# Attention in a macaron block: reciprocal chain moved ahead, and three small TensorE products in other tile modes

## The reference

```
x = x + 0.5 * ffn(layernorm(x), w_gate, w_up, w_down)   # FP4 block quantization of inputs and weights
x = x + attn(layernorm(x), ...)                         # 16 heads of 64
x = x + 0.5 * ffn(layernorm(x), w_gate, w_up, w_down)

attn(x):  q, k, v = x@w_q, x@w_k, x@w_v     # split in 16 heads
          p = softmax(q k^T / 8)            # over 512 keys
          o = p v
          y = o @ w_proj + b_proj + x;  return layernorm(y) * gamma + beta
```

## Time and profile before

| what | value |
|---|---|
| median of 3 runs | 3089.62 us |
| the profiled execution's own time | 3096.16 us |
| its span | 3094.4 us |
| PE busy | 2483.0 us, 80% |
| DVE busy | 1587.0 us, 51% |
| POOL busy | 1408.8 us, 46% |
| ACT busy | 1284.9 us, 42% |
| mean granted TensorE clock | 0.892 |

### The profile page before, as it was taken

How to read it: one execution, slowest core, us unless ns; L and a number is a source line. 1 busy time by engine, 2 the same in 40 slices (tenths; PEclk the granted TensorE clock), 3 DMA queues, 4 the chain that set the end, 5 groups by cost and what they waited for, 6 DMA issues and landing times. The chain is left out here.

```text
span 3094.4 us, 38590 instructions
## 1 busy us (share of the span) xinstructions
PE 2483.0 (80%) x12073; PEld 1317.5 (43%) x12073; DVE 1587.0 (51%) x2806; ACT 1284.9 (42%) x2363; POOL 1408.8 (46%) x1268
## 2 busy tenths in 40 slices
PE   4677688888888888888888888888888888846776
PEld 2455444444444444444444444444444444424444
DVE  6888544444444444444444444444444444339996
ACT  3555344343334333434334344443443444325553
POOL 3666355444445444444444444444454444435554
PEclk9877699898889888999999899999998999868778
DMA  3000000000000000000000000000000000000010
GB/s 108 28 27 20 17 1 1 2 2 2 2 1 1 1 2 1 2 1 2 1 1 2 2 2 1 2 1 1 1 2 1 2 1 2 1 18 24 21 30 17
DMA packets 143530, 27.70 MB, mean 9 GB/s; under 512 B 112064, under 2 KB 138880, under 8 KB 143360
## 3 DMA queue, kind: packets, MB, share of 16 engines
q1 hardware_dynamic: 143360, 25.43, 4.4%
HBM read 15.42 MB, written 8.39 MB: 8 GB/s over the span
## 5 line engine op out<-in xcount | busy, mean ns | idle before, releaser
L902 DVE TENSOR_REDUCE nmax<-pX 128x1 f32<-128x512 f32 x1024 | 659.3, 686 | 654.7 <-PE pX L967 476.5
L827 POOL TENSOR_TENSOR ES<-E 128x512 f32<-128x512 f32 x256 | 323.6, 1286 | 1087.6 <-ACT E L854 1087.6
L854 ACT ACTIVATE E<-pS 128x512 f32<-128x512 f32 x1024 | 555.9, 594 | 620.6 <-PE pS L956 614.0
L832 POOL TENSOR_TENSOR ES<-ES,E 128x512 f32<-128x512 f32 x512 | 644.8, 1281 | 238.4 <-ACT E L854 236.0
L982 PE MATMUL pO<-E,VA 128*64 128x512 f32 x2048 | 588.0, 654 | 0.0
L1033 PE MATMUL pR<-RROW,sel 128*128 128x512 f32 x128 | 78.0, 610 | 342.1 <-DMA RROW<-RC 341.3
L916 DVE TENSOR_TENSOR ON<-OT,pR 128x512 f32<-128x512 f32 x128 | 87.9, 687 | 405.5 <-PE pR L1033 405.5
L956 PE MATMUL pS<-QH,KH 64*128 64x512 f32 x1024 | 275.7, 535 | 7.2 <-issue 7.2
L941 PE MATMUL pM<-xc,wqk 128*128 128x512 f32 x768 | 266.8, 461 | 7.3 <-DMA wp<-in_L_attn_w_proj 5.2
L861 ACT ACTIVATE QH<-pM 128x512 fp32r<-128x512 f32 x128 | 76.6, 598 | 441.4 <-PE pM L941 441.4
L941 PEld LDWEIGHTS pM<-xc,wqk 128*128 128x128 f32 x768 | 155.6, 217 | 164.9 <-issue 133.9
(11 more groups left out here) (156 smaller groups left out, 3565.2 us busy)
## 6 DMA issues: line engine op xcount, KB each, us to landing
RROW<-RC SPq DMA_DIRECT2D x512, 2.0 KB, 2.0
Fxin<-in_L_attn_x SPq DMA_DIRECT2D x16, 256.0 KB, 2.8
Y<-in_L_attn_x SPq DMA_DIRECT2D x16, 256.0 KB, 5.0
x<-Fxout SPq DMA_DIRECT2D x16, 256.0 KB, 2.0
LC<-LROW SPq DMA_DIRECT2D x256, 2.0 KB, 2.1
Lx1in<-x SPq DMA_DIRECT2D x16, 256.0 KB, 2.7
out<-Lxout SPq DMA_DIRECT2D x16, 256.0 KB, 2.9
w_raw<-in_L_attn_w_q SPq DMA_DIRECT2D x1, 512.0 KB, 5.6
```

Of the source, the lines that this page charges most:

```text
L827: g.tensor_tensor(ES[par][hd][:, :], E[0][hd][:, :], E[1][hd][:, :], ALU.add).then_inc(s_add, 1)
L832: g.tensor_tensor(ES[par][hd][:, :], ES[par][hd][:, :], E[s][hd][:, :], ALU.add).then_inc(s_add, 1)
L854: a.activation(E[s][hd][:, :], pS[hd][:, :], ACT.Exp).then_inc(s_exp, 1)
L902: v.tensor_reduce(nmax[:, 64 * hd + t:64 * hd + t + 1], pX[hd][:, :], AX.X, ALU.max, negate=True).then_inc(s_max, 1)
```

## The change

Five edits, all in the attention.

1. VectorE: the reciprocal of pair i-2 moves from the end of step 2 to step 1, behind ON and ahead of KL.
2. GpSimd: both parts of RC move to the head of step 2, ahead of the ES sums of that step.
3. TensorE: the spread product of pair i-3 moves from step 0, behind `times_v`, to step 1, between `for_maxima` and `times_v`. It takes 64 rows of `sel` and RROW (of which four are not zero) in place of 128. VectorE's ON moves from step 0 to step 1 with it.
4. TensorE: the transpose of the maxima becomes two float32 matmuls with the identity, each on 64 columns of `nmax`, into the two halves of pR.
5. TensorE: the output projection's four matmuls (128 columns of weights) become eight, each with 64 columns of ON, into the two halves of pY.

```diff
 POOL
-                        if s == 3 and there(i - 2, NP):
+                        if s == 2 and there(i - 2, NP):
                             pool.wait_ge(s_rec, i - 1)
                             g.tensor_tensor(RC[par][:, 0, :, :], REC[par][:, :, :], ...ones..., ALU.mult).then_inc(s_rhi, 1)
+                            pool.wait_ge(s_rhi, i - 1)
+                            g.tensor_tensor(RC[par][:, 1, :, :], REC[par][:, :, :], RC[par][:, 0, :, :].bitcast(F32),
+                                            ALU.subtract).then_inc(s_rlo, 1)
...
-                        if s == 3 and there(i - 2, NP):
-                            (the low part, behind the ES sums)
 DVE
-                        if s == 0 and there(i - 3, NP):   (ON, ahead of QL)
+                        if s == 1 and there(i - 3, NP):
+                            dve.wait_ge(s_rb, i - 2)
+                            wait(dve, s_proj, i - 3)
+                            v.tensor_tensor(ON[:, :], OT[(p - 3) % 4][:, :], pR[:, :], ALU.mult).then_inc(s_norm, 1)
+                        if s == 1 and there(i - 2, NP):
+                            dve.wait_ge(s_lc, 32 * (i - 1))
+                            v.reciprocal(REC[par][:, :, :], LC[par][:, :, :]).then_inc(s_rec, 1)
...
-                        if s == 2 and there(i - 2, NP):   (the reciprocal, behind SH)
 PE, project
-                        ins = pe_.matmul(pY[:, t * 128:(t + 1) * 128], ON[:, t * 128:(t + 1) * 128], wp[:, po, :], ...)
+                        for n in range(2):
+                            ins = pe_.matmul(pY[half(n), t * 128:(t + 1) * 128],
+                                             ON[:, t * 128 + 64 * n:t * 128 + 64 * n + 64], wp[:, po, :], ...)
 PE, body
+                        if s == 1 and there(i - 3, NP):   (ahead of times_v)
+                            pe.wait_ge(s_rrow, 64 * (i - 2))
+                            pe.wait_ge(s_lrow, min(i - 1, NP) if isinstance(i, int) else i - 1)
+                            pe_.matmul(pR[:, :], sel[0:64, :], RROW[0:64, :], start=True, stop=True).then_inc(s_rb, 1)
...
-                        if s == 0 and there(i - 3, NP):   (the same with sel[:, :], RROW[:, :], behind times_v)
...
-                            pe_.transpose(pR[:, 0:128], nmax[:, :], ident[:, :]).then_inc(s_mrow, 1)
+                            for hd in range(2):
+                                ins = pe_.matmul(pR[half(hd), 0:128], nmax[:, half(hd)], ident[:, :], start=True, stop=True)
+                            ins.then_inc(s_mrow, 1)
```

More of the change, by code:

```diff
@@ L832, in body @@
                                 g.tensor_tensor(ES[par][hd][:, :], ES[par][hd][:, :], E[s][hd][:, :], ALU.add).then_inc(s_add, 1)
-                        if s == 3 and there(i - 2, NP):
-                            pool.wait_ge(s_rhi, i - 1)
-                            g.tensor_tensor(RC[par][:, 1, :, :], REC[par][:, :, :], RC[par][:, 0, :, :].bitcast(F32),
-                                            ALU.subtract).then_inc(s_rlo, 1)
                         if s == 1 and p == 1 and there(b + 1, B) and there(b, B):
@@ L912, in body @@
                             maxima(i + 2, s - 2)
[L913 to L916, removed]
                         if s == 0 and there(i + 2, NP):
@@ L930, in body @@
                                             ALU.mult).then_inc(s_sh, 1)
-                        if s == 2 and there(i - 2, NP):
-                            dve.wait_ge(s_lc, 32 * (i - 1))
-                            v.reciprocal(REC[par][:, :, :], LC[par][:, :, :]).then_inc(s_rec, 1)
                 steps(dve, body)
@@ L1003, in project @@
                     for t in range(T):
-                        ins = pe_.matmul(pY[:, t * 128:(t + 1) * 128], ON[:, t * 128:(t + 1) * 128], wp[:, po, :],
-                                         start=False, stop=po == PAIRS - 1 and t == T - 1)
+                        for n in range(2):
+                            ins = pe_.matmul(pY[half(n), t * 128:(t + 1) * 128],
+                                             ON[:, t * 128 + 64 * n:t * 128 + 64 * n + 64], wp[:, po, :],
+                                             start=False, stop=po == PAIRS - 1 and t == T - 1)
                     ins.then_inc(s_proj, 1)
@@ L1029, in body @@
                             row_sums(i - 1, 1 - p % 2)
[L1030 to L1033, removed]
                         if s == 0 and there(i + 2, NP):
```

## The result

The changed kernel takes 2609.47 us (median of 4 runs, 2608.15 to 2610.65) against 3092.61 us before (median of 4, 3083.85 to 3102.7). The ratio is 0.8437, 95% interval 0.8409 to 0.8464: 483 us less. The forecast was 2598.

The account below looks back on a forecast made before the run. PE was taken as the bound, with one hole per pair. 124 pairs at 14.50 us gave 1798 against 2279.6; with the ends -497 from the span 3094.4, so 2597.4, forecast 2598 us, range 2572 to 2720.

Parts of the forecast that it names:

- likeliest case: The whole kernel: the forecast of 2598 us holds, own range 2580 to 2630, chance 0.70.
- The hole: PE's wait for RROW before the spread product, 2.7 us per pair: RROW issued 6.6 us earlier, product 2.1 later, wait gone.
- The clock: TensorE in the attention: the half-clock stretches go with the hole, the whole 1.2 us per pair gained.
- Transpose, projection, spread product: PE, per pair: transpose net -0.04 us, projection 0 with full overlap of the halves, spread product net 0.
- Rival A: Transpose and projection: the 64-column halves don't overlap at 128 columns, +1.1 us per pair, 2735 us; chance 0.08.
- The sum: Attention pairs: 14.50 us each with the batch product, 124 pairs 1798 us against 2279.6, -481.6; total -497.
- The batch's input product: PE's product that adds the batch's input, every eighth pair: about 0.9 us, so 0.11 per pair on average.
- the last three pairs: The last three of the 124 pairs: no V or Q work, shorter by some 4 us in all.
- The tail: Pair 127 and the three bodies behind it: 5 us off the pair and 6 off the rest, between 0 and 18.
- B: TensorE in the attention: the clock still falls, 2745 us if all of it stays, 2670 if half; chance 0.08.
- C: A shorter pair finds a new wait, at the held maxima or ACT's queue: 0.3 to 1 us per pair, 2635 to 2720; chance 0.12.
- D: DVE and POOL queues: LC over 3.4 us late holds up PE; at 8 us late 19.1 per pair, 3170 us; chance 0.02.

Follow-up runs that it names:

- The filled hole: Eleven extra products of 512 columns that nobody reads, ahead of the spread product, against the kernel before: 2979.41 us, ratio 0.9623.
- both of these kernels: The changed kernel with extra DMAs on SP ahead of the two LC DMAs: twelve took 2843.68 us, five took 2615.59 us.

## Why the prediction was right

The mechanism was right and most sizes nearly so; the time is 11 us over the forecast, inside the likeliest case's own range. That the sum came so near is in part luck, as its terms below show.

- *The hole.* RROW is issued 6.6 us earlier was the claim; RC leaves POOL at step 2 + 2.0 (1509.17 - 1507.15), as worked out, and the wait is gone. (Before, 1552.63 was the start of its low part, which left at 1552.84; so it is 6.8 us.) What I didn't ask is whether this alone does it. It does (edits 1 and 2: 2611 us); the later place of the product was worth nothing on top. 6.6 us are more than the hole of 2.7; the 2.1 us of the product's later place are less, and that kernel took 2731 us.
- *The clock.* 1.2 us per pair was taken in full; the clock is 1.00. The filled hole shows that the cause was PE's idle time in the hole, no other part of the load, and gives at least 1.0 us for it. 0.06 of the 1.2 was no clock: in the kernel before, too, PE idles at the six turns of the loop (see the sum below).
- *Transpose, projection, spread product.* -0.04, 0 and 0 were the terms, in step 2 3.50 against 3.46 measured and in step 1 3.50 against 3.49. Rival A, no overlap of short halves, didn't come; nor did the 0.1 us per pair of the Trainium skill's 62 ns per MATMUL (TensorE: Matmul & The Clock Gate, Part 1), which would hold with hardware decode off: sixteen MATMULs and a change of mode passed in 0.97 us, where sixteen times 62 ns and the 0.1 of the change make 1.09, an estimate from that page.
- *The sum.* From pair 3 to pair 127 it gave 1798 less 4 = 1794 us, and 1800.0 came. Two terms were missing or too small. The batch's input product I took at 0.11 us per pair, 13.6 in all; with edits 4 and 5 it stands alone in its mode between column tiles and costs 1.20, 16 x 1.20 = 19.2: 5.6 us more. And the loop over two batches has an edge that I had not read in the trace. At six places PE stands idle between the V projection and the next scores, as here in the changed kernel and then in the kernel before:

```profile
725.51 0.97 PE L940 MATMUL pM<-wv,xc 128*128 128x512 f32 x3
728.06 0.50 PE L955 MATMUL pS<-QH,KH 64*128 64x512 f32 x2 [1.58 <-issue]
```

```profile
805.53 0.50 PE L956 MATMUL pS<-QH,KH 64*128 64x512 f32 x2 [1.43 <-issue]
```

  These six pairs take 15.6 to 16.0 us, together 8.8 us over the others. Against both stand the steps, 14.33 (median) in place of 14.39, -7.4 us, and the last three pairs, 4.9 us shorter and not 4. So 1794 + 5.6 + 8.8 - 7.4 - 0.9 = 1800: a sum that comes near because its terms cancel.
- *The tail.* 40.7 us before, 29.8 after the first scores of pair 127: -10.9, where I took -11.
- *The rest.* The two feed-forward blocks were 2 to 3 us longer in this execution, the second one 354.6 us in place of 352.5; no run here isolates why.
- *The rivals.* B fell with the clock. C came in no form. D is a real mechanism. The reciprocal waits from 3.3 us on, as D said, but PE loses less than D said: next to nothing at 3.2 us late, 1.7 us per pair at 7.6. The LC DMAs take 2.1 us (median) to land in both of these kernels.

## What to carry to other kernels

A hole of under 3 us in front of one small product, once in 18 us, cost twice: itself, and the TensorE clock behind it, so look at the producer's place in the queues before shaping the consumer. Here two moved lines on two engines with slack brought the whole 483 us, and the three edits on the bound engine brought nothing that a run could tell. Once PE was at 99.5%, only grouping products by tile mode still paid: 4 us for one product per batch moved to where its mode already ran.

## What the runs showed of the hardware

- Filling an idle gap of TensorE with useless products made the program 3.8% faster (2979 against 3102 us), since the clock stayed at 2.4 GHz. A gap of 0.33 to 0.35 us per 15 us never brought the clock down, one of 2.7 us per 18 us brought the mean to 0.93. In between it depends: single gaps of 1.4 to 2.0 us were followed by a stretch at 1.2 GHz in 6 of 16 cases in the kernel with edit 3 alone, the six of 1.2 to 1.6 us at the loop's turns of the changed kernel never.
- A change of tile mode costs 0.1 us (PV to the full-array transpose 1.01 us, PV to the row sums, in the same mode, 0.91), and a full-array product alone between 64-row and 64-column products 0.2 us more than the 64-row form.
- Float32 products of 128 columns in 64-column halves run side by side: sixteen instructions in 0.97 us, where eight full-width ones took 0.99. Halving the width neither gained nor lost.
- Each of the six turns of the hardware loop left TensorE idle for 1.2 to 1.6 us in the changed kernel and for 1.0 to 1.5 in the kernel before, and the trace names no semaphore that it waited for. What it waited for isn't shown.
